# Copying a gather's row numbers one column behind each indirect transfer, in a three-layer graph kernel

## The reference, cut to what matters

```python
def gat_conv(h, src, dst, fc_w, attn_l, attn_r, bias, heads, out_feats):
    feat = (h @ fc_w.T).reshape(n, heads, out_feats)
    el = jnp.sum(feat * attn_l, axis=-1)
    er = jnp.sum(feat * attn_r, axis=-1)
    e = jax.nn.leaky_relu(el[src] + er[dst], 0.2)
    ...
    a = ex / ssum[dst]
    rst = jax.ops.segment_sum(feat[src] * a[..., None], dst, num_segments=n)
...
# the last round: queries, keys and values, 4 heads of 64
mod_k = K[src] + 0.2 * rel[:, None, :]
scores = jnp.einsum('ehd,ehd->eh', Q[dst], mod_k) / D ** 0.5
...
agg = jax.ops.segment_sum(w[:, :, None] * V[src], dst, num_segments=N)
```

## Time and profile before

| | |
|---|---|
| time, median of 3 runs | 3384.52 us (3381.06 to 3429.43) |
| span of the profiled execution | 3410.9 us; no separate time is given for this execution |
| busy shares of the span | PE 48%, weight loads 34%, DVE 45%, ACT 12%, POOL 48% |
| indirect transfers | 1664, each one POOL instruction |
| copies of row numbers | 104, 16 columns each |
| DMA, mean | 85 GB/s |

### The profile page before, as it was taken

One profiled execution on the slowest core, in us unless ns is written; L12 is line 12 of the kernel. 1 busy time (PEld: TensorE's weight loads), 2 busy tenths in 40 slices (PEclk: granted clock), 3 DMA queues, 4 the chain that ended last, 5 costly groups with the idle time before them and its releaser, 6 DMA issues.

```text
span 3410.9 us, 30471 instructions
## 1 busy us (share of the span) xinstructions
PE 1633.6 (48%) x7573; PEld 1176.0 (34%) x7574; DVE 1540.5 (45%) x2386; ACT 406.0 (12%) x809; POOL 1641.8 (48%) x1791
## 2 busy tenths in 40 slices
PE   3624334335367342443345945655566233333455
PEld 2313323223255332332233434444344222322343
DVE  3225454536464772232235535545565432322368
ACT  0100000000012000000001433333333100000012
POOL 0240656455502715655660065665656756556600
PEclk8855767667688556766667967777777566666765
DMA  1532323223303522322321343343333323223211
GB/s 33 125 92 55 86 70 92 63 82 82 80 29 99 165 77 83 91 82 82 89 85 34 98 115 98 104 106 98 105 99 102 99 79 91 82 82 89 85 29 61
DMA packets 166449, 289.97 MB, mean 85 GB/s; under 512 B 37842, under 2 KB 113035, under 8 KB 166411
## 3 DMA queue, kind: packets, MB, share of 16 engines
q0 software_dynamic: 79872, 219.91, 22.7%
q1 hardware_dynamic: 86539, 69.66, 8.1%
HBM read 272.74 MB, written 16.68 MB: 85 GB/s over the span
## 4 chain that ended last, share of the span: by engine, by line
another core or an unknown queue 36%; DVE 23%; PE 21%; issue 13%; DMA 4%; DVEq 1%; SPq 1%; ACT 0%; POOL 0%; ACTq 0%; POOLq 0%
PE ps L918 5%; DVE arena L1688 5%; PE ps L870 3%; DMA arena<-rows_block_dst 3%; DVE arena L1931 2%; PE ps L1077 2%; DVE arena L1580 2%; DVE scores L1570 2%; DVE arena L1588 1%; PE ps L797 1%; PE ps L1054 1%; PE ps L1003 1%; DVE arena L1924 1%; DVE arena L1498 1%
## 5 line engine op out<-in xcount | busy, mean ns | idle before, releaser
L722 POOL DMA_INDIRECT row_space<-tab_feat,index_slot x832 | 816.5, 981 | 687.4 <-issue 322.5
L918 PE MATMUL ps<-arena 128*128 128x257 f32 (+1 forms) x1664 | 481.9, 457 | 702.2 <-DVE arena L1692 504.8
L918 PEld LDWEIGHTS ps<-arena 128*128 128x128 f32 x1664 | 379.3, 233 | 804.7 <-issue 731.6
L722 POOL DMA_INDIRECT row_space<-tab_k,index_slot x416 | 393.9, 947 | 255.8 <-issue 162.1
L722 POOL DMA_INDIRECT row_space<-tab_v,index_slot x416 | 403.4, 970 | 229.1 <-issue 128.4
L1683 DVE TENSOR_TENSOR arena<-ps,block_dst 128x1024 f32<-128x1024 f32 x104 | 127.0, 1222 | 809.0 <-remote 681.9
L1003 PE MATMUL ps<-arena 128*128 128x265 f32 x832 | 249.8, 463 | 102.8 <-DVE ps L1914 49.5
L870 PE MATMUL ps<-row_space,arena 128*128 x832 | 294.0, 514 | 0.0
L1580 DVE TENSOR_TENSOR arena<-row_space,ps 128x1024 f32<-128x1024 f32 x104 | 126.8, 1219 | 322.0 <-remote 223.7
L1195 ACT COPY acc<-ps 128x265 f32<-128x265 f32 (+2 forms) x75 | 28.2, 376 | 1786.8 <-remote 1064.6
L1003 PEld LDWEIGHTS ps<-arena 128*128 128x128 f32 x832 | 189.1, 233 | 149.0 <-issue 107.9
(11 more groups left out here) (316 smaller groups left out, 2120.1 us busy)
## 6 DMA issues: line engine op xcount, KB each, us to landing
arena<-rows_block_dst SPq DMA_DIRECT2D x156, 128.0 KB
row_space<-tab_feat,index_slot POOLq DMA_INDIRECT x832
arena<-rows_src_low SPq DMA_DIRECT2D x52, 128.0 KB
arena<-rows_type SPq DMA_DIRECT2D x52, 128.0 KB
row_space<-tab_k,index_slot POOLq DMA_INDIRECT x416
row_space<-tab_v,index_slot POOLq DMA_INDIRECT x416
arena<-in_x_t SPq DMA_DIRECT2D x50, 128.0 KB, 2.2
tab_feat<-arena SPq DMA_DIRECT2D x25, 132.0 KB, 1.8
```

Of the source, the lines that this page charges most:

```text
L722: nc.gpsimd.indirect_dma_start((wide_rows[:, s] if n == 0 else row_slots[s])[:, g, :], None, table, bass.IndirectOffsetOnAxis(ap=index_slo ...
L918: last = nc.tensor.matmul(ps[:, SUM_BANKS:2 * SUM_BANKS][:, bass.ds(bs[g], 1), 0:width].rearrange("p a d -> p (a d)"), onehot[:, s % 2, g, ...
```

## The change

Each transfer is followed by a copy of one column: behind transfer g of slot s, POOL copies column g of the slot two further on. The wait for the landing of that slot's earlier gather moves to the head of each slot, and with it the wait on `pool_step`, which now asks for the copies of slot s (made during slot s-2). Ahead of a pass, POOL makes 16 one-column copies for slots 0 and 1, where there was one copy of 16 columns. In all there are 1664 copies of one column for 104 of 16. The transfers, their order, the rings and everything on the other engines stay.

```diff
-                def indices(u, s):
-                    for k in (s, s + 1):
-                        pool.wait_ge(gathered[k], u * (16 * GROUP) + (uses(n, k) * 16 * GROUP))
+                def index(u, s, g):
                     nc.gpsimd.tensor_copy(
-                        index_slot[:, s:s + 2].rearrange("p s g -> p (s g)"),
-                        src_i[:, bass.ds(u * (ring * GROUP) + s * GROUP, 2 * GROUP)]).then_inc(pool_step, 1)
+                        index_slot[:, s, g:g + 1],
+                        src_i[:, bass.ds(u * (ring * GROUP) + s * GROUP + g, 1)]).then_inc(pool_step, 1)
+
+                def landed(u, s):
+                    pool.wait_ge(gathered[s], u * (16 * GROUP) + (uses(n, s) * 16 * GROUP))

                 def gather(u, s, ends):
-                    if s % 2 == 0:
-                        pool.wait_ge(pool_step, u * (ring // 2) + (s // 2 + 1 + step.n))
-                    elif not ends:
-                        indices(u + (s + 1) // ring, (s + 1) % ring)
+                    ahead = u + (s + 2) // ring, (s + 2) % ring
+                    if not ends:
+                        landed(*ahead)
+                    pool.wait_ge(pool_step, u * (ring * GROUP) + ((s + 1) * GROUP + step.n))
...
                         ).then_inc(gathered[s], 16)
-
-                indices(0, 0)
+                        if not ends:
+                            index(*ahead, g)
+
+                for s in range(2):
+                    landed(0, s)
+                    for g in range(GROUP):
+                        index(0, s, g)
                 with nc.gpsimd.Fori(0, turns) as u:
                     for s in range(ring):
                         gather(u, s, False)
                 for s in range(rest):
-                    gather(turns, s, s + 1 == rest)
-                step.add(GROUPS // 2)
+                    gather(turns, s, s + 2 >= rest)
+                step.add(ITEMS)
```

## The result

The kernel after took 3346.50 us (median of 5 runs, 3332.59 to 3397.22), the kernel before 3384.52 beside it (5 runs, 3372.67 to 3429.43). The ratio is 0.9896, with a 95% interval of 0.9863 to 0.9930: 1% faster, and less than the 2% from which the prediction calls a kernel faster. The profiled execution of after is the slowest of its five, 3397.22 us, some 50 above their median, and that of before is 26 above its own. So the stages are compared by their cycles first, and by their sums with care.

What follows compares the result with a forecast made beforehand. It took PE's semaphore raises, late while transfers follow closely, to bound the kernel. sum2 and sum3 -30, score3 -18, sum1 -8, pass starts +4 make -52: 3384.5 to 3332 us; range 3050 to 3460, the forecast's own 3280 to 3390.

Steps and rivals of the forecast that it cites:

- the mechanism of a backlog: Something serves each transfer in 1.39 us, falls behind by 0.14 us with each, and admits PE's raises after catching up.
- the late raises: PE's semaphore raises reach DVE late while transfers follow closely; in sum2 both engines idle 20.7 us with work done.
- The copy: One-column copy behind each transfer: about 190 ns, step between transfers 1.32 to 1.33 us, +133 us of POOL time.
- The line 0.6 + 1.39n: Time in us from a run's first transfer to DVE's release, for n transfers.
- sum2 and sum3: Five slots a cycle (60.4 us) or six (71.5) instead of four; 12.4 to 12.0 us a slot, -30 us.
- The window that was to bring the fifth slot: In sum2's cycle, DVE gets PE's raises without loss for 12 to 13 transfers, 16 us, instead of some 6.
- score3: Three slots a cycle in 36.1 us, where two took 24.8: -0.4 x 48 = -18 us.
- sum1: Chunks take 57.9 or 52.1 us; between none and seven long ones turned, 0 to -41, taken as -8 us.
- Pass starts: 15 more copies ahead of each of four passes, 3 us each; hidden in passes 0 and 1, +4 us taken.
- Rival C: Slower: the copy's `pool_step` raise queues like a transfer's 16, 0.087 us each; +134, 3518 us, or 3450 for half; chance 0.17.
- Rival A: Spacing suffices, PE's raises flow, stalls go and POOL bounds: 2910 us, or 3150 for half of the runs; chance 0.32.
- Nearly all of it hides: The copies' added POOL time (+133 us, less 8) hides: a run of 32 ends at 42.6 us, release at 45.1.

Runs made afterwards that it cites:

- e8: Kernel before with each transfer split into two of 64 rows, so twice the raises for each item: 4647.65 us (one execution), before 2814 us.
- e5: Kernel after, unchanged, run again where before took 2806 us: 2911.70 us, 1.0380 of before.
- e6: Kernel before, unchanged, run again for its trace: 2804.55 us in the profiled execution.
- the first trace: Profiled execution of the unchanged kernel before, from the runs with a median of 3384.52 us; this execution was 26 us above that median.
- e11: Kernel before without copies of row numbers or waits on `pool_step`, gather loops written out, transfers reading src_i directly: 3428.19 us, ratio 1.0048.
- the second to fourth comparison: Three later sets of experiments, each on a different chip with the kernel before beside them, which took 2806, 2806 and 2814 us.

## Why the prediction was nearly right, and what it did not see

The forecast was 3332 us, with a difference of -52; measured were 3346.5 and -38. The time came out near, and the mechanism of a backlog held with the late raises, but the parts did not come as forecast. In the two profiled executions, which are 15.4 us apart, from the end of one stage to the end of the next on DVE: in after score1 is 7.9 us shorter, score2 6.5, sum2 13.3 and sum3 8.8, while sum1 is 14.3 longer and score3 6.8. These are single executions 26 and 50 us above their medians, so what made up the 38 us is shown for the cycles of sum2 and sum3 alone, and that the whole came out so near is in part luck. By its steps:

- **The copy**: 190 ns and a step of 1.32 to 1.33 were forecast, 191 ns and 1.326 came.
- **The line 0.6 + 1.39n**: held at each step and with no copy at all (table above). That the 16 raises of a transfer are the thing served stays an inference; e8, aimed at it, missed, and the 0.092 us between PE's raises is only near it.
- **sum2 and sum3**: the fifth slot came, with cycles of 60.4 forecast and 60.7 measured. The sixth never came. The two passes shrink by 17.4 (714.2 to 696.8) and 2.4 us (636.9 to 634.5) between POOL's first and last transfer: 20 for a forecast of 30.
- **The window that was to bring the fifth slot** did so only in part. The raises do come earlier: the fourth slot starts 8.4 to 14.3 us into a run in after, 13.5 to 20.0 in before. But the fifth was to start within a stretch of 16 us without loss. In fifteen of the sixteen runs of 40 in sum2 and sum3 it starts 23 to 38 us into the run, behind a wait of 11 to 22 us, when a single raise comes through (18.44 us in the cycle shown). The prediction had no such raise in it; the agreement of 60.4 and 60.7 rests on the line alone, which gives the cycle once the number of slots is known.
- **score3**: here the step failed. A third slot in a cycle was to give 18 us. Sixteen of 21 cycles stayed at two slots (24.89). Five have three, of which two took the forecast 36 us and three 40.7 to 42.4, 13.6 to 14.1 a slot, so that the five together take 13.2 a slot and gain nothing. POOL's pass is 5.4 us shorter (653.9 to 648.5), but DVE's first to last L1580 takes 683.6 us for 671.5. The ring of pass 2 has four slots; whether that keeps the cycles at two was not tested.
- **sum1**: -8 forecast. POOL's pass 0 is 8.0 us shorter (798.1 to 790.1), but the stage is not: DVE's first to last L1931 takes 658.4 us for 644.1. The agreement in the pass is luck: two chunks took 48.8 and nearly all others 56 to 58, where 57.9 and 52.1 had stood side by side. The wait moved from one hop to PE to another: L1846 191.8 to 31.9 us, L1874 83.7 to 250.4 (lines of before).
- **Pass starts**: +4 forecast. From the end of pass 2 to the start of pass 3 it is 10.4 us for 1.1, from pass 0 to pass 1 164.4 for 147.8. In e5 and e6, without late raises, these are 2.1 for 1.1 and 149.3 for 148.6. So the copies cost 1 us, as the row says, 1.95 us for all sixteen ahead of pass 3; the rest of the 10.4 is a wait for DVE to free a slot, as at the end of any run:

```profile
2594.15 1.95 POOL L700 COPY index_slot<-src_i 128x1 int32<-128x1 int32 x16
2604.52 0.97 POOL L722 DMA_INDIRECT row_space<-tab_v,index_slot  x1 [8.42 <-DVEq L1306]
```

  The longer way from pass 0 to pass 1 goes with sum1, whose last run of transfers is one of 32 in after and one of 8 in before.
- **Rival C** (the copy's raise queues with the others, 3518): refuted by its own sign. Runs of 32 were to release DVE later than 47.9 us; those of after do so at 45.34 in the median, and 40 transfers lie on the old line.
- **Rival A** (the raises flow): not here. But its arithmetic for POOL as the bound gave 2910, and after takes 2911.7 on a chip without late raises. What it did not see is that before then takes 2806.

**The step that was missing** is the premise. I read the late raises as a property of this kernel's transfers, and they are absent on three chips with the same instructions at the same durations. "Nearly all of it hides" named the cover rightly, the lag behind the transfers, and also named what follows if it goes: POOL is next, with +133 - 8 = 125 us. Measured were 105.5. The step grew by 0.075 us for the 0.08 forecast, which is 8 us of the difference, and the first 64 transfers of passes 0 and 1 hide beside score1 and score2. The Trainium skill's GPSIMD Engine Reference (§7, performance pitfalls) advises batching small read commands, indices among them. The estimate from its figure was 85 ns for each copy; where no raises are late the traces have 105.5 / 1560 = 68 ns, so they agree with it in size. Where raises are late the kernel with the small copies was 1% faster, against the advice.

## What to carry to other kernels

Work put between two commands of an engine costs the step that it adds, not its own duration (0.075 us for a copy of 0.191 here), and whether that step is on the path can depend on the chip or its condition. Where the chain gives a third of the span to "another core or an unknown queue", take the same kernel's trace from a second chip before tuning to it: this change gave -1% in one place and +3.8% in another. Where POOL's transfers bound the passes, the number of transfers counts, neither their rows (64 rows 0.91 us, 128 rows 0.95) nor their bytes (half of them: 2806 us for 2814).

## What the runs showed of the hardware that was not expected

- The same program took 2806 to 2814 us in three comparisons and 3384 to 3429 in two, at the same durations of its instructions. The difference stands in waits on semaphores that PE raises: DVE waits 1259 us on "remote" in the first trace (1097 at three lines) and not at all in e6, where it waits 812 us at four lines for the gathered rows instead.
- The data is not late. From the start of a transfer to the end of its last DMA packet it is 2.42 us in the median, in the first trace of before as in e6. But the first trace holds only 5066 events of the 26624 raises that 1664 transfers make on the `gathered` semaphores, that of e6 26551; e11 has 5029, and each of the ten traces of the second to fourth comparison holds over 99% of its raises. That fits with something that passes on semaphore raises, and not the data, being at its limit there; that the profiler alone lost these events is not excluded. What it is and why it differs is not shown.
- Eight one-column copies in a row take 1.01 us, 0.13 each, where one alone takes 0.19.
- When late raises of PE come through, they come 0.092 us apart.
- Beside DVE's L1498 in score2 (L1503 in after), a one-column copy takes 1.06 us for 0.19.
